# Query and key parts in DRAM: one copy each, and 4 KB rows read into the stacks by twelve transfers

## The reference

```
x = x + conv_attention(ctx, ctx, norm(x))       # layer 0: outer products of 8 x 8 per head, long convolution, times query
x = x + ffn_ternary(norm(x))                    # layer 0: rounded weights and activations, 256 -> 1024 (gated) -> 256
x = x + cross_attention(norm(x), ctx)           # layer 1: q = Wq t + bq, k = Wk s + bk, 16 heads of 8 channels,
                                                #   dot = q.k/sqrt(8), masked, softmax over s, times v
x = x + topk_mixture(norm(x))                   # layer 1: 512 logits, the 32 largest, softmax, 32-wide genes, tanh(down)*xn*up
```

## Time and profile before

| | us |
|---|---|
| median of 3 runs | 585.58 (579.73 to 590.35) |
| the profiled execution | 580.47 |
| its span | 578.7 |
| GpSimd / ScalarE / VectorE / TensorE busy in it | 377.2 / 350.3 / 453.2 / 463.3 |

### The profile page before, as it was taken

How to read it: one execution, slowest core, us unless ns; L and a number is a source line. 1 busy time by engine, 2 the same in 40 slices (tenths; PEclk the granted TensorE clock), 3 DMA queues, 4 the chain that set the end, 5 groups by cost and what they waited for, 6 DMA issues and landing times.

```text
span 578.7 us, 11242 instructions
## 1 busy us (share of the span) xinstructions
PE 463.3 (80%) x3587; PEld 258.3 (45%) x3587; DVE 453.2 (78%) x885; ACT 350.3 (61%) x607; POOL 377.2 (65%) x692
## 2 busy tenths in 40 slices
PE   1686699997987988888989889898887888777452
PEld 1575477765754544444544344443443333322110
DVE  4586479998669979799899899798988997874341
ACT  1469524333121677788788788788876786776231
POOL 6467389998977757777778778776664762343222
PEclk9888889999879999999899999899999998996755
DMA  6970110101551257357354573546745765210100
GB/s 197 372 174 19 48 28 29 22 7 56 89 120 24 80 79 163 94 99 150 91 102 124 100 144 100 90 120 127 157 103 111 137 143 96 50 24 19 50 9 19
DMA packets 93935, 54.49 MB, mean 94 GB/s; under 512 B 16611, under 2 KB 93603, under 8 KB 93877
## 3 DMA queue, kind: packets, MB, share of 16 engines
q1 hardware_dynamic: 93876, 53.78, 41.0%
HBM read 35.84 MB, written 17.42 MB: 92 GB/s over the span
## 4 chain that ended last, share of the span: by engine, by line
PE 24%; issue 21%; POOL 20%; POOLq 14%; DVE 7%; ACT 6%; DMA 4%; SPq 3%; DVEq 0%; ACTq 0%
PE pair L280 7%; POOL kv L949 5%; PE bank L501 4%; POOL w_raw L1026 4%; ACT cT L1310 3%; POOLq L977 3%; POOLq L42 3%; DVE w_int L1656 2%; POOL w_int L45 2%; POOLq L975 2%; PE pair L488 2%; PE bank L393 2%; PE pair L472 2%; DMA yT<-in_x 2%; POOLq L40 2%
## 5 line engine op out<-in xcount | busy, mean ns | idle before, releaser
L1656 DVE TENSOR_REDUCE w_int<-pair 128x4 f32<-128x1024 f32 x128 | 155.2, 1213 | 28.9 <-PE pair L472 28.3
L1310 ACT ACTIVATE cT<-pair 128x1024 f32<-128x1024 f32 x128 | 131.0, 1023 | 38.2 <-PE pair L488 35.8
L280 PE MATMUL pair<-kv,toep 128*128 128x256 f32 x384 | 102.8, 413 | 11.7 <-POOL kv L949 8.0
L280 PEld LDWEIGHTS pair<-kv,toep 128*128 128x128 f32 x384 | 76.0, 207 | 28.2 <-issue 8.4
L488 PE MATMUL pair<-w_raw,KS 57*128 57x256 bf16 x512 | 51.2, 279 | 33.7 <-ACT cT L1310 23.7
L949 POOL TENSOR_TENSOR kv<-cT 128x512 f32<-128x512 f32 x64 | 66.2, 1041 | 17.9 <-PE pair L280 12.4
L501 PE MATMUL bank<-cT,v_aug 128*32 128x256 f32 x1024 | 73.4, 406 | 0.2 <-ACT qT L1318 0.2
L1481 DVE TENSOR_TENSOR prod<-pair,qT 128x512 f32<-128x512 f32 x64 | 43.8, 685 | 23.5 <-PE pair L280 22.7
L472 PE MATMUL pair<-KS,w_raw 54*128 54x256 bf16 x512 | 50.3, 275 | 11.2 <-DVE w_int L1656 10.8
L488 PEld LDWEIGHTS pair<-w_raw,KS 57*128 57x128 bf16 x512 | 16.9, 95 | 72.9 <-ACT cT L1310 54.1
L1257 ACT ACTIVATE w_raw<-bank,st 128x512 f32<-128x512 f32 x32 | 22.0, 688 | 39.0 <-PE bank L394 39.0
(11 more groups left out here) (174 smaller groups left out, 941.9 us busy)
## 6 DMA issues: line engine op xcount, KB each, us to landing
w_raw<-scr_q SPq DMA_DIRECT2D x32, 192.0 KB
KS<-scr_k SPq DMA_DIRECT2D x32, 192.0 KB
scr_q<-w_int SPq DMA_DIRECT2D x16, 192.0 KB, 2.5
scr_k<-w_int SPq DMA_DIRECT2D x16, 192.0 KB, 2.6
scr_o<-qT SPq DMA_DIRECT2D x64, 36.0 KB
yT<-in_x SPq DMA_DIRECT2D x4, 512.0 KB, 7.6
ctx_all<-in_ctx SPq DMA_DIRECT2D x4, 512.0 KB, 8.1
x_b<-in_x SPq DMA_DIRECT2D x16, 128.0 KB, 4.9
```

What stands on the lines that cost most here:

```text
L280: mm = pe.matmul(bank[:, lh * n:(lh + 1) * n], toep[:, h, (lh - sh) * P:(lh - sh + 1) * P], rhs[:, sh, :], start=(sh == 0), stop=(sh == lh))
L1310: act.activation(probs[g % 4].rearrange("p j l -> p (j l)"), SC[:], ACT.Exp).then_inc(s("scores_free"), 1)
L1656: dve.tensor_reduce(neg_max[:, :, 2 * g:2 * g + 2].rearrange("p t j -> p j t"), M[:].rearrange("p (j t s) -> p j t s", t=KL, s=L), AX.X, A ...
```

## The change

write_qk_parts writes each of the three parts of q and of k once, into one DRAM tensor scr_qk[k, q or k, part, 16 channel pairs, 8 groups, 256], in which the eight groups of a stack row lie side by side (4 KB in one piece). load_stacked_qk reads rows of 4 KB; since the terms repeat parts, each half and operand takes three transfers (runs of 3, 2 and 1 terms), the ones for QS with a step of 0 over the terms of a run. The semaphore counts go from 8 to 16 transfers.

```diff
-    scr_q = nc.dram_tensor("scr_q", [2, P, NT, L], BF16, kind="Internal").ap()
-    scr_k = nc.dram_tensor("scr_k", [2, P, NT, L], BF16, kind="Internal").ap()
+    scr_qk = nc.dram_tensor("scr_qk", [2, 2, 3, 2 * HD, GRP, L], BF16, kind="Internal").ap()
...
-                    pe.wait_ge(s(f"qs{b % 3}_loaded"), 16 * 8 * (b // 3 + 1))
+                    pe.wait_ge(s(f"qs{b % 3}_loaded"), 16 * 16 * (b // 3 + 1))
...
                 if b >= 2:
-                    sp.wait_ge(s(f"qs{(b - 2) % 3}_loaded"), 16 * 8 * ((b - 2) // 3 + 1))
-                first = 0
-                for run in (3, 2, 1):
-                    terms = slice(first, first + run)
-                    sp.dma_start(scr_q[k, :, terms, :], qk_parts[k][:, TERM_Q[first], 0:1, :].broadcast_to([P, run, L])
-                                 ).then_inc(s(f"parts{k}_written"), 16)
-                    sp.dma_start(scr_k[k, :, terms, :], qk_parts[k][:, 0:run, 1, :]).then_inc(s(f"parts{k}_written"), 16)
-                    first += run
+                    sp.wait_ge(s(f"qs{(b - 2) % 3}_loaded"), 16 * 16 * ((b - 2) // 3 + 1))
+                for t in range(3):
+                    for n in range(2):
+                        sp.dma_start(scr_qk[k, n, t].rearrange("r g l -> g r l"), qk_parts[k][:, t, n, :]
+                                     ).then_inc(s(f"parts{k}_written"), 16)
...
                 sp.wait_ge(s(f"parts{k}_written"), 16 * 6 * (b // 2 + 1))
-                stacked = "(g j c) t l -> j (c t) g l"
+                part, row = 2 * HD * GRP * L, GRP * L
                 for j in range(2):
-                    rows = slice(HALF * j, HALF * j + ROWS)
-                    sp.dma_start(QS[n][rows, :, :], scr_q[k].rearrange(stacked, g=GRP, j=2)[j]).then_inc(loaded, 16)
-                    sp.dma_start(KS[n][rows, :, :], scr_k[k].rearrange(stacked, g=GRP, j=2)[j]).then_inc(loaded, 16)
+                    first = 0
+                    for run in (3, 2, 1):
+                        rows = slice(HALF * j + HD * first, HALF * j + HD * (first + run))
+                        q_at = (2 * k * 3 + TERM_Q[first]) * part + HD * j * row
+                        k_at = (2 * k + 1) * 3 * part + HD * j * row
+                        sp.dma_start(QS[n][rows, :, :], bass.AP(scr_qk.tensor, q_at, [[0, run], [row, HD], [1, GRP * L]])
+                                     ).then_inc(loaded, 16)
+                        sp.dma_start(KS[n][rows, :, :], bass.AP(scr_qk.tensor, k_at, [[part, run], [row, HD], [1, GRP * L]])
+                                     ).then_inc(loaded, 16)
+                        first += run
```

## The result

The changed kernel takes 676.17 us (median of 4 runs, 672.1 to 676.96) against 583.31 us of the kernel before beside it: ratio 1.160, 95% interval 1.151 to 1.170. The forecast was 620, with a range up to 650. The direction and the chain of waits hold; the size was more than twice what I worked out, 93 us in place of 37.

A forecast was written before the change was run, and what follows sets the result against it. Engine hand-overs in each iteration were taken to bound the kernel. The profiled 580.5 us plus 37 us of stack waits gave 617.5; half the 5.1 us median offset made it 620, range 588 to 650.

The forecast's parts named there:

- What bounds the kernel, and the relay: Engine hand-overs set the time; a late stack holds TensorE's maxima and transpose, then the max rows, then SyncE's next round.
- Writes, issue unchanged: SyncE's six writes of parts a batch keep their issue time, 3.2 us in all, with fewer bytes.
- Twelve loads, 6.8 us to issue: SyncE issues twelve stack loads in place of four: 6.8 us against 1.8, +4.9 us a batch.
- Hidden until iteration 17, up to 3 us late in 18 to 22: SyncE's idle time covers the added issue until iteration 17; later write_attention slips up to 3 us, adding nothing behind late stacks.
- The wide spread: Rival, chance 0.14: partition side alone sets the engines, stacks land on time, SyncE's late issue costs 12 us; 581 to 595.
- Engines: 3, 2 and 8: Stack loads of runs 3, 2 and 1 use only 3, 2 and 8 engines, set by the DRAM side's outermost dimension.
- perhaps 8: The six writes perhaps use 8 engines, 2.7 us behind the stacks in iterations 18 to 22, costing nothing.
- Landing 12.8 us after the first issue: First engine carries 68 of 192 rows, 11.0 us plus 1.8; less slacks of 135.2 in all, maxima wait 44 us.
- Five sixths, as something is caught up: Of 44 us of waits by the maxima, five sixths, 37 us, reach the time; other engines catch up the rest.
- nothing caught up: Upper case of the few-engines range: all 44 us of waits count, with a few more queueing losses 648 us.

The follow-up runs named there:

- experiment 2: The kernel before with each of its four stack loads cut into three of 16 partitions, same layout and bytes: 585.78 us, ratio 1.010.
- experiment 1: The changed kernel with the two outer dimensions of each stack load exchanged, so that 8 is outermost: 597.61 us, ratio 1.028.
- experiment 3: The changed kernel with 20 unused matmuls on TensorE before its stack wait, batches 2 to 15: 656.35 us, ratio 1.123; its table splits iterations at the first maxima.
- the best version of the change: The kernel of experiment 1 with SyncE's six writes moved behind load_attention in iterations 18 and up: 594.12 us, ratio 1.015.
- the four long transfers: The changed kernel with repeated terms written out by twelve writes, each stack half read as 48 rows of 4 KB in one transfer: 617.77 us, ratio 1.064.

## Why the prediction was wrong

*What bounds the kernel, and the relay.* Right: maxima, transpose, max rows, SyncE's next round are tied, and the stall passes through all of them.

*Writes, issue unchanged.* Off: 0.57 us each, 3.8 us for the six in place of 3.2. Their target has one more dimension than before.

*Twelve loads, 6.8 us to issue.* They take 7.3. *Hidden until iteration 17, up to 3 us late in 18 to 22.* Near where stacks are on time: experiment 2, with plain pieces, lost 4 to 6 us where 7 were expected. The wide spread was put at 581 to 595, and experiment 1, which comes nearest to it, measured 597.6, just above.

*Engines: 3, 2 and 8.* Right, by the counts and by experiment 1. This was the step on which the sign hung. The engines of the writes, "perhaps 8", are 8 by the counts too.

*Landing 12.8 us after the first issue.* Failed in size: the maxima start 14.8 us after it on average. The rate of 25.4 GB/s was right for a steady engine: the median row takes 0.159 us, 25.8 GB/s. But 15% of the rows take over 0.2 us, and the mean is 0.192 us (21.3 GB/s), so that the rows take 12.7 us from first to last in place of 11.0; start and completion are 2.1 us in place of 1.8. So the waits are 71 us in place of 44; 14 x 14.8 - 135.2 = 72, the same sum with the measured landing.

*"Five sixths, as something is caught up".* Failed, and this is the step that was wrong in kind. Nothing was caught up: 71 us of waits cost 93. TensorE loses half of its clock during the wait and runs the next 6 us with it, on the path. The table of experiment 3 shows it: besides the 69 us of later stacks, the way from the maxima to the next stack issue grew by 21 us (in the iteration from 364 us it is 15.4 us, 13.5 before), and keeping TensorE busy during the wait takes just these away. The forecast had no term for this, and put a discount of a sixth where an addition of nearly a third was due.

*The range.* It ended at 650 because its upper end allowed "nothing caught up", and no more. A stall that makes other work slower has no place in a sum that only lets it be hidden.

## What to carry to other kernels

Look at a transfer's outermost dimension on both sides before looking at its row length or its bytes: here the same rows, bytes and transfers cost 77 us more with 3 and 2 outermost than with 8, and it was two brackets. A falling mean DMA share beside a growing wait for a DMA is how it showed. When a new wait hits TensorE, price the clock too: here about 5 us of idling were followed by some 6 us at half the clock, and 20 us of it showed in the time, since TensorE's next results are waited for. And ask first whether anyone waits for the transfer that is to be improved; here nobody did, and the best version of the change (1.015) still loses, at least in part by the issue time that it adds.

## What the runs showed of the hardware

Issue time on SyncE's queue depends on the form of the transfer: 0.29 to 0.46 us for 8 partitions, 0.43 for 16 plain ones, 0.6 to 0.77 for a source of two dimensions over 16 or 24 partitions, 0.57 for the writes into a target of two dimensions. A 4 KB row took 0.159 us on an engine in steady work (25.8 GB/s) and 0.192 us on average in the changed kernel; with 16 engines in the four long transfers the average was 0.33 us. The order of issue of narrow and wide transfers moved the start of the maxima by 1.3 us on average (12.8 to 11.5 us after the first issue) with the same rows on each engine.
